# One-hot comparisons of a histogram shared between VectorE and GpSimd, and a hardware loop written out

## The chip, the cores and the metric

The kernel runs on one core of a Trainium2 chip. The metric is the device time of one execution in microseconds, as the median of several runs. Lower is better.

## The reference, cut to what matters

The program is a stack of four graph layers over 50,000 nodes and 25,000 edges. `src` and `dst` are the ends of each edge. The part that matters here is the degree count that the first layer asks for, and a row number for the compact tables:

```
loops = arange(n)
src   = concat([edge_index[0], loops])
deg   = segment_sum(ones, src, num_segments=n)
norm  = where(deg > 0, rsqrt(deg), 0)
```

Every later layer sums over `dst`. For that the kernel also needs to know, for each node, whether it has edges that end there, and its place among the nodes that have. So two histograms over the nodes are wanted: one of `src` (side 0) and one of `dst` (side 1).

## The kernel before, in words

The edges are padded to 25,600, which are T = 200 tiles of P = 128 edges. The function `prelude` is one stage of the program. It runs after the edge lists have been brought into SBUF (`edges_in`) and before the stage `node_rows`, whose first loads read what the prelude writes (`info_s`). Between two stages stands a barrier of all engines (in `run`, lines 2572 to 2580).

A histogram is computed as a sum of matrix products. A node number is split into a high part (number shifted right by 9, fewer than 98 values) and a low part (number and 511). For one tile and one side, the high parts become a one-hot matrix of 128 edges by 128 columns (`hi1`), and the low parts a one-hot matrix of 128 edges by 512 columns (`lo1`). Both are float16. TensorE multiplies the transposed first by the second and accumulates the 128x512 result in PSUM (`ph[:, side, :]`) over all tiles. Each one-hot matrix is one `tensor_scalar` with `is_equal`: a row of counting numbers (`g.iota_lo`, float16) against a value per partition, which is a column of `part` (float32, in SBUF).

Before, all four comparisons of a tile are made by VectorE, in the order hi side 0, lo side 0, hi side 1, lo side 1 (lines 500 and 501). The buffers `hi1` and `lo1` hold PER = 8 tiles. Two semaphores order the two engines: `s_cmp` counts finished pairs of comparisons, and TensorE waits for it before each product (line 539); `s_mm` counts finished products, and VectorE waits for it before it overwrites a buffer (line 499). Both engines run a hardware loop of 25 turns with 8 tiles written out in it. The counts in the semaphores are worked out from the loop register. GpSimd has no work in this stage.

After the loop TensorE closes the two sums (line 542), VectorE reads them (lines 504 and 505), and a chain of some 20 small steps over VectorE, ScalarE and TensorE makes the degree norm, a running count and the turned weights. The SP queue meanwhile loads weights, and at the end writes `info_s`.

`wait_alone(g, eng, sem, value)` is a wait followed by an increment of a semaphore that nobody waits for; it keeps the wait an instruction of its own.

Of the kernel before, what the change touches and what calls it, by code (L numbers as in the profile page):

```python
# [11 lines left out]
ALU = mybir.AluOpType  # L12
# [6 lines left out]
P = 128  # L19
# [3 lines left out]
T = EP // P  # L23
# [48 lines left out]
def wait_alone(g, eng, sem, value):  # L72

    eng.wait_ge(sem, value)
    eng.sem_inc(g.state.waits, 1)
# [315 lines left out]
def prelude(nc, g):  # L391
# [2 lines left out]
    s_ld, s_z, s_zd, s_big, s_bl, s_pe, s_v, s_d, s_w = (g.sem("wt_" + n) for n in ("ld", "z", "zd", "big", "bl", "pe", "v", "d", "w"))  # L394
    s_zh, s_cmp, s_mm, s_all, s_vec, s_deg, s_norm, s_sum, s_pre, s_row, s_out, s_turned = (
        g.sem("nn_" + n) for n in ("zh", "cmp", "mm", "all", "vec", "deg", "norm", "sum", "pre", "row", "out", "turned"))
    PER = 8
    with ctx:
        sb = lambda n, s, d=F32: ctx.enter_context(nc.sbuf_tensor(n, s, d))
# [9 lines left out]
        part = sb("nn_partf", [P, 2, 2, T])  # L409
# [36 lines left out]
        @block.sync  # L446
        def _(sp):
            for dest, src in loads:
                sp.dma_start(dest, src).then_inc(s_ld, 16)
            sp.wait_ge(s_z, 1)  # L450
            for k, a in ((2, g.vec1[:, 0]), (3, g.vec2[:, 0])):
                sp.dma_start(cols[0:HFULL, k, :], a[0:HFULL * HL].rearrange("(p w) -> p w", w=HL)).then_inc(s_vec, 16)
                sp.dma_start(cols[HFULL:HR, k, 0:HLEFT], a[HFULL * HL:N].unsqueeze(0)).then_inc(s_vec, 16)
            sp.dma_start(g.w1big_s, zero[:, 0:P]).then_inc(s_zd, 16)
            sp.dma_start(g.w2big_s.rearrange("(k p) n -> p k n", p=P), zero[:, P:3 * P].rearrange("p (k n) -> p k n", k=2)).then_inc(s_zd, 16)
            for dest, src in heads:
                sp.dma_start(dest, src).then_inc(s_ld, 16)
            sp.wait_ge(s_zd, 32)
            with nc.allow_non_contiguous_dma(reason="small weights laid out once"):
                for dest, src in pieces:  # L460
                    sp.dma_start(dest, src).then_inc(s_big, 16)
            sp.wait_ge(s_big, 16 * len(pieces))
            sp.dma_start(g.w1big[:, :], g.w1big_s).then_inc(s_bl, 16)
            sp.dma_start(g.w2big[:, :, :], g.w2big_s.rearrange("(k p) n -> p k n", p=P)).then_inc(s_bl, 16)
            sp.wait_ge(s_row, 1)
            sp.dma_start(g.info_s.rearrange("(p w) k -> p (w k)", w=HL), rows[:, :, :].rearrange("p w k -> p (w k)")).then_inc(s_out, 16)
            sp.wait_ge(s_w, 1)
            sp.dma_start(g.h_tab[EP:EP + 1, :], g.b0_row[0:1, :]).then_inc(s_d, 16)
            sp.wait_ge(s_out, 16)
            sp.wait_ge(s_d, 16)  # L470

        @block.scalar
        def _(a):
# [3 lines left out]
            a.wait_ge(s_norm, 1)  # L477
            a.activation(cols[:, 0, :], cols[:, 0, :], ACT.Exp, scale=-0.5).then_inc(s_norm, 1)

        @block.vector  # L480
        def _(v):
            v.memset(att[:, :, :], 0.0)
            v.memset(ones[:, :], 1.0)
            v.memset(cols[:, :, :], 0.0)
            v.memset(line[:, :], 1.0)
            v.memset(total[:, :], 0.0)
            v.memset(zero[:, :], 0.0).then_inc(s_z, 1)
            v.memset(zh[:, :], 0.0).then_inc(s_zh, 1)
            c = Chain(v, s_v)
            v.tensor_copy(both_i[:, 0, :], g.src_f[:, :])  # L490
            c.step(v.tensor_copy(both_i[:, 1, :], g.dst_f[:, :]))
            v.tensor_scalar(part_i[:, 0, :, :], both_i[:, :, :], 9, None, ALU.logical_shift_right)
            c.step(v.tensor_scalar(part_i[:, 1, :, :], both_i[:, :, :], HL - 1, None, ALU.bitwise_and))
            c.step(v.tensor_copy(part[:, :, :, :], part_i[:, :, :, :]))
            v.sem_inc(s_cmp, 2 * PER)
            with v.Fori(0, T // PER) as i:
                for k in range(PER):
                    for side in range(2):
                        v.wait_ge(s_mm, i * 2 * PER + 2 * k + side + 1)
                        v.tensor_scalar(hi1[:, k, side, :], g.iota_lo[:, 0:P], part[:, 0, side, bass.ds(i * PER + k, 1)], None, ALU.is_equal)  # L500
                        v.tensor_scalar(lo1[:, k, side, :], g.iota_lo[:, :], part[:, 1, side, bass.ds(i * PER + k, 1)], None,
                                        ALU.is_equal).then_inc(s_cmp, 1)
            v.wait_ge(s_all, 2)
            v.tensor_scalar(cols[:, 0, :], ph[0:HR, 0, :], 1.0, None, ALU.add).then_inc(s_deg, 1)
            c.step(v.tensor_copy(hist[:, :], ph[0:HR, 1, :]))
            v.tensor_reduce(total[0:HR, :], hist[:, :], AX.X, ALU.add).then_inc(s_sum, 1)
            v.wait_ge(s_pre, 1)
            c.step(v.tensor_copy(first[:, :], pp[0:HR, :]))
            c.step(v.tensor_tensor_scan(upto[:, :], line[:, :], hist[:, :], first[:, :], ALU.mult, ALU.add))
            c.step(v.scalar_tensor_tensor(cols[:, 1, :], hist[:, :], 0.5, upto[:, :], ALU.is_gt, ALU.mult))  # L510
            v.wait_ge(s_norm, 2)
            v.wait_ge(s_vec, 64)
            v.tensor_copy(rows[:, :, :].rearrange("p w k -> p k w"), cols[:, :, :]).then_inc(s_row, 1)
            v.wait_ge(s_ld, 16 * (len(loads) + len(heads)))
            c.step(v.tensor_scalar(g.b1_rows[:, :], g.b1_rows[:, :], 0.0, None, ALU.max))
            v.wait_ge(s_pe, 18)
            for n in range(18):
                turned = v.tensor_copy(wT[:, n, :], ps[:, n // 4, n % 4, :])
            turned.then_inc(s_turned, 1)
            v.wait_ge(s_bl, 32)  # L520
            v.tensor_scalar(g.w1big[:, :], g.w1big[:, :], float(1 / np.sqrt(MUL)), None, ALU.mult)
            v.tensor_scalar(g.w2big[S:2 * S, 0, :], g.w2big[S:2 * S, 0, :], float(1 / np.sqrt(3.0)), None, ALU.mult)
            c.step(v.tensor_scalar(g.wfc2[:, :], g.wfc2[:, :], float(1 / np.sqrt(HID)), None, ALU.mult))
            v.wait_ge(s_pe, 18 + 3)
            v.tensor_copy(g.wq[:, :], pq)
            v.tensor_copy(g.wa[:, :], pa)
            v.tensor_tensor(g.bu_rows[:, :], bu[:, :], pb, ALU.subtract)
            v.tensor_scalar(g.b0_row[0:1, :], p0, 0.0, None, ALU.max).then_inc(s_w, 1)

        @block.tensor  # L530
        def _(pe):
            pe.wait_ge(s_zh, 1)
            for side in range(2):
                pe.matmul(ph[:, side, :], zh[:, 0:P], zh[:, :], start=True, stop=False)
            pe.sem_inc(s_mm, 2 * PER)
            with pe.Fori(0, T // PER) as i:
                for k in range(PER):
                    for side in range(2):
                        pe.wait_ge(s_cmp, i * 2 * PER + 2 * PER + 2 * k + side + 1)
                        pe.matmul(ph[:, side, :], hi1[:, k, side, :], lo1[:, k, side, :], start=False, stop=False).then_inc(s_mm, 1)  # L540
            for side in range(2):
                pe.matmul(ph[:, side, :], zh[:, 0:P], zh[:, :], start=False, stop=True).then_inc(s_all, 1)
            pe.wait_ge(s_sum, 1)
            pe.matmul(pp, g.lower[:, :], total[:, :], start=True, stop=True).then_inc(s_pre, 1)
            pe.wait_ge(s_z, 1)
            pe.wait_ge(s_ld, 16 * (len(loads) + len(heads)))
            for n in range(16):
                pe.transpose(ps[:, n // 4, n % 4, :], g.wr[:, n, :], g.ident[:, :]).then_inc(s_pe, 1)
            for n in range(2):
                pe.transpose(ps[:, 4, n, :], g.w12[:, n * P:(n + 1) * P], g.ident[:, :]).then_inc(s_pe, 1)  # L550
            pe.wait_ge(s_turned, 1)
            for n in range(16):
                last = pe.matmul(pq[:, n:n + 1], wT[:, n, :], g.att_q[:, n // R_:n // R_ + 1], start=True, stop=True)
            last.then_inc(s_pe, 1)
            for k in range(2):
                last = pe.matmul(pa, wT[:, 16 + k, :], att[:, k, :], start=(k == 0), stop=(k == 1))
            last.then_inc(s_pe, 1)
            for k in range(2):
                pe.matmul(pb, ones[:, :], g.wu[:, k, :], start=(k == 0), stop=(k == 1))

            pe.matmul(p0, g.b1_col[:, 0:1], g.ident[:, :], start=True, stop=True).then_inc(s_pe, 1)
# [2078 lines left out]
```

## Time and profile before

| | |
|---|---|
| runs | 4418.27, 4420.27, 4423.72 us; median 4420.27 |
| profiled execution | 4440.37 us, its span 4438.7 us |
| mean granted TensorE clock in it | 0.821 of full speed |
| busy share of the span | VectorE 77%, TensorE 68%, ScalarE 49%, GpSimd 47% |
| the stage in question | about 45 to 244.8 us of the span; the histogram loop 50.8 to 220.9 us |

Busy shares are averages over many stages that have different limits. What a change in one stage is worth is read from the rows of that stage.

### The profile page before, as it was taken

The numbers are of one execution on the slowest core, as the hardware profiler recorded it, in microseconds if no ns is written. First come the engines' busy times: TensorE is split into PE (matmuls) and PEld (weight loads), VectorE is DVE, ScalarE is ACT, GpSimd is POOL, SyncE is SP. The second block draws the span as 40 slices with busy tenths as digits, with TensorE's granted clock in tenths as the row PEclk, the third lists the DMA queues.
The fourth block names the chain that finished last, engine by engine and source line by source line (L and its number), as shares of the span: only waits on it lengthen the run. The fifth ranks groups of instructions, "written<-read, shape, count | busy, mean of one in ns | idle before, by whom it ended". The sixth has DMA issues, their size and how long they took to land. (4 is left out here: it accounts for less than half of the span.)

```text
span 4438.7 us, 67467 instructions
## 1 busy us (share of the span) xinstructions
PE 3028.4 (68%) x12342; PEld 1728.7 (39%) x12342; DVE 3396.4 (77%) x9927; ACT 2153.8 (49%) x5600; POOL 2094.9 (47%) x2258
## 2 busy tenths in 40 slices
PE   5956644444445999478999224888886999706886
PEld 1255533333332444123444112555553666503443
DVE  6978858888886888675555685888884666697997
ACT  0057756776662222162222355766664666504554
POOL 0057767777774555006553002555544555203566
PEclk9967767677767999788999555989887999958998
DMA  2079967767773222174222496444444565503332
GB/s 51 2 210 285 286 207 230 230 223 228 230 225 89 64 62 61 40 229 86 60 62 47 131 245 164 116 118 122 118 120 131 196 200 194 170 0 112 113 112 87
DMA packets 621013, 627.71 MB, mean 141 GB/s; under 512 B 167332, under 2 KB 494590, under 8 KB 614468
## 3 DMA queue, kind: packets, MB, share of 16 engines
q1 hardware_dynamic: 572900, 523.78, 39.4%
q0 software_dynamic: 48000, 102.76, 9.6%
q14 instruction: 84, 0.69, 0.0%
q8 instruction: 29, 0.48, 0.0%
HBM read 333.97 MB, written 296.91 MB: 142 GB/s over the span
## 5 line engine op out<-in xcount | busy, mean ns | idle before, releaser
L1410 PE MATMUL r_pM<-r_masked,wr 128*128 128x512 f32 x1600 | 750.0, 622 | 55.2 <-DVE r_masked L1361 31.5
L1361 DVE SCALAR_TENSOR_TENSOR r_masked<-r_typ,r_hT 128x512 f32<-128x512 f32 x800 | 493.8, 689 | 241.4 <-ACT r_hT L1388 164.0
L1410 PEld LDWEIGHTS r_pM<-r_masked,wr 128*128 128x128 f32 x1600 | 308.7, 199 | 426.7 <-issue 326.1
L1252 PE MATMUL e_pY<-ident,e_agg 128*128 128x128 f32 x400 | 134.0, 438 | 370.3 <-issue 246.7
L741 POOL DMA_INDIRECT q_rows<-nr,row_x x200 | 258.0, 1290 | 209.4 <-PE q_pT L590 149.8
L2431 POOL DMA_INDIRECT out<-o_base,o_at_o x200 | 241.6, 1208 | 162.1 <-DVE o_base L2472 93.8
L741 POOL DMA_INDIRECT r_xs<-h_tab,r_at_s x200 | 216.1, 1080 | 87.7 <-issue 51.8
L741 POOL DMA_INDIRECT r_xs<-tab,r_at_s x200 | 214.1, 1071 | 89.1 <-issue 52.3
L1252 PEld LDWEIGHTS e_pY<-ident,e_agg 128*128 128x128 f32 x400 | 106.9, 327 | 382.3 <-issue 305.1
L590 PE MATMUL g_pT<-ident,g_hT 128*128 128x128 f32 x400 | 96.0, 384 | 226.5 <-ACT g_hT L1792 177.1
L1006 PE MATMUL na_pZ<-w,na_aT 128*128 128x128 f32 x784 | 159.6, 386 | 117.7 <-ACT na_aT L988 117.6
L741 POOL DMA_INDIRECT i_hs<-hr,i_at_s x200 | 194.5, 972 | 87.9 <-issue 50.4
L741 POOL DMA_INDIRECT e_zs<-xz,src_c x200 | 191.1, 955 | 70.1 <-issue 60.7
L2239 ACT ACTIVATE q_eo<-q_pO,b 128x512 f32<-128x512 f32 x196 | 134.8, 688 | 181.9 <-PE q_pO L2274 147.9
L741 POOL DMA_INDIRECT e_zd<-xz,dst_c x200 | 192.8, 964 | 53.5 <-issue 48.5
L1006 PEld LDWEIGHTS na_pZ<-w,na_aT 128*128 128x128 f32 x784 | 147.3, 289 | 131.0 <-ACT na_aT L988 113.1
L1388 ACT ACTIVATE r_hT<-r_pS 128x512 f32<-128x512 f32 x100 | 59.6, 596 | 273.8 <-PE r_pS L590 261.3
L2274 PE MATMUL q_pO<-q_nT,w 128*128 128x512 f32 x392 | 187.7, 602 | 5.2 <-issue 5.2
L590 PEld LDWEIGHTS g_pT<-ident,g_hT 128*128 128x128 f32 x400 | 61.6, 191 | 301.3 <-ACT g_hT L1792 118.3
L1098 POOL TENSOR_TENSOR e_zh<-e_z,e_hh 128x512 f32<-128x512 f32 x98 | 139.0, 1438 | 75.0 <-ACT e_hh L1201 60.8
L1903 POOL COPY i_at_s<-row_x 128x4 int32 (+1 forms) x50 | 9.4, 187 | 347.8 <-PEq L715 327.8
L2208 DVE TENSOR_TENSOR q_base<-q_pU,q_base 128x512 f32<-128x512 f32 x98 | 67.8, 692 | 132.5 <-PE q_pU L2283 121.0
(418 smaller groups left out, 9048.8 us busy)
## 6 DMA issues: line engine op xcount, KB each, us to landing
xz<-na_xz SPq DMA_DIRECT2D x49, 1040.0 KB
r_typ<-vec_s SPq DMA_DIRECT2D x100, 256.0 KB
g_al<-alpha_s SPq DMA_DIRECT2D x100, 256.0 KB, 3.9
na_xz<-in_x SPq DMA_DIRECT2D x49, 512.0 KB
tab<-na_x SPq DMA_DIRECT2D x49, 512.0 KB
e_xin<-tab SPq DMA_DIRECT2D x49, 512.0 KB
hr<-e_hh SPq DMA_DIRECT2D x49, 512.0 KB
zh_s<-e_zh SPq DMA_DIRECT2D x49, 512.0 KB
```

The lines of the kernel that those rows point to most:

```text
L590: last = pe.transpose(ps[:, j * P:(j + 1) * P], y4[:, j, :], g.ident[:, :])
L741: pool.indirect_dma_start(dest[:, j, :], None, table, bass.IndirectOffsetOnAxis(ap=index[:, j:j + 1], axis=0), element_offset=first).then_ ...
L1006: last = pe.matmul(pZ[p.slot(2)][m][:, j * P:(j + 1) * P], aT[:, m * J + j, :], g.w0[:, :], start=True, stop=True)
L1098: pool.tensor_tensor(zh[s][:, of(m), :], z[s][:, of(m), :], hh[s][:, of(m), :], ALU.add).then_inc(nd.zz, 1)
L1252: pe.matmul(pY[s][:, cols], agg[s][:, cols], g.ident[:, :], start=True, stop=False)
L1361: v.scalar_tensor_tensor(masked[:, r, :], typ[d.slot(4)][:, :], float(r), hT[d.slot(2)][:, :], ALU.is_equal, ALU.mult).then_inc(ev.mk, 1)
L1388: a.activation(hT[b.slot(2)][:, :], pS[b.slot(2)][:, :], ACT.Relu).then_inc(ev.hT, 1)
L1410: pe.matmul(pM[s][:, :], g.wr[:, layer * R_ + r, :], masked[:, r, :], start=(r == 0), stop=(r == R_ - 1)).then_inc(ev.mm, 1)
L2208: v.tensor_tensor(rows, four(pU[m][:, :]), rows, ALU.add).then_inc(nd.fo, 1)
L2239: a.activation(eo[:, m, k, :], pO[m][:, k, :], ACT.Exp, bias=g.b12[:, k:k + 1])
L2274: last = pe.matmul(pO[m][:, k, :], g.w12[:, k * P:(k + 1) * P], nT[:, of(m), :], start=True, stop=True)
L2431: pool.indirect_dma_start(g.out, bass.IndirectOffsetOnAxis(ap=at_o[s][:, j:j + 1], axis=0), base[s][:, j, :], None, bounds_check=N - 1, oo ...
```

## The change

GpSimd takes the narrow comparison of side 1 (`hi1[:, k, 1, :]`) of every tile. VectorE keeps hi side 0, lo side 0 and lo side 1. A semaphore `s_parts` tells GpSimd once that `part` is ready, and `s_hi` counts its comparisons. TensorE waits for `s_hi` as well before each product of side 1. The hardware loops on VectorE and TensorE become Python loops over all 200 tiles, so that every instruction is in the program once per tile, with constants for the semaphore values and for the column of `part`. GpSimd's part is written out in the same way. The number of buffers stays 8.

```diff
+    s_parts, s_hi = g.sem("nn_parts"), g.sem("nn_hi")
...
+        @block.gpsimd
+        def _(pool):
+            wait_alone(g, pool, s_parts, 1)
+            for t in range(T):
+                if t >= PER:
+                    wait_alone(g, pool, s_mm, 2 * (t - PER) + 2)
+                pool.tensor_scalar(hi1[:, t % PER, 1, :], g.iota_lo[:, 0:P], part[:, 0, 1, t:t + 1], None, ALU.is_equal).then_inc(s_hi, 1)
...
-            v.sem_inc(s_cmp, 2 * PER)
-            with v.Fori(0, T // PER) as i:
-                for k in range(PER):
-                    for side in range(2):
-                        v.wait_ge(s_mm, i * 2 * PER + 2 * k + side + 1)
-                        v.tensor_scalar(hi1[:, k, side, :], g.iota_lo[:, 0:P], part[:, 0, side, bass.ds(i * PER + k, 1)], None, ALU.is_equal)
-                        v.tensor_scalar(lo1[:, k, side, :], g.iota_lo[:, :], part[:, 1, side, bass.ds(i * PER + k, 1)], None,
-                                        ALU.is_equal).then_inc(s_cmp, 1)
+            v.sem_inc(s_parts, 1)
+            for t in range(T):
+                k = t % PER
+                for side in range(2):
+                    if t >= PER:
+                        v.wait_ge(s_mm, 2 * (t - PER) + side + 1)
+                    if side == 0:
+                        v.tensor_scalar(hi1[:, k, side, :], g.iota_lo[:, 0:P], part[:, 0, side, t:t + 1], None, ALU.is_equal)
+                    v.tensor_scalar(lo1[:, k, side, :], g.iota_lo[:, :], part[:, 1, side, t:t + 1], None, ALU.is_equal).then_inc(s_cmp, 1)
...
-            pe.sem_inc(s_mm, 2 * PER)
-            with pe.Fori(0, T // PER) as i:
-                for k in range(PER):
-                    for side in range(2):
-                        pe.wait_ge(s_cmp, i * 2 * PER + 2 * PER + 2 * k + side + 1)
-                        pe.matmul(ph[:, side, :], hi1[:, k, side, :], lo1[:, k, side, :], start=False, stop=False).then_inc(s_mm, 1)
+            for t in range(T):
+                k = t % PER
+                for side in range(2):
+                    if side == 1:
+                        pe.wait_ge(s_hi, t + 1)
+                    pe.wait_ge(s_cmp, 2 * t + side + 1)
+                    pe.matmul(ph[:, side, :], hi1[:, k, side, :], lo1[:, k, side, :], start=False, stop=False).then_inc(s_mm, 1)
```

## Rows read from the trace of the kernel before

**Rows 1.** Busy time in the histogram loop, by engine, then clock, DMA share, GB/s

```profile
50.80:221.20 170.40, 155.83 (x401) 38.34 (x402) 170.09 (x800) 0.00 (x0) 0.00 (x0) 1.00 0.07 9
```

**Rows 2.** Groups of instructions in the loop: busy us, mean ns, then idle before

```profile
L540 PE MATMUL nn_ph<-nn_lo,nn_hi 128*128 128x512 f16 x400 | 156.0, 395 | 15.5 <-DVE nn_lo L501 1.5
L501 DVE TENSOR_SCALAR nn_lo<-iota_lo,nn_partf 128x512 f16<-128x512 f16 x400 | 134.2, 335 | 0.0
L500 DVE TENSOR_SCALAR nn_hi<-iota_lo,nn_partf 128x128 f16<-128x128 f16 x400 | 94.9, 237 | 0.5 <-DVE nn_partf L494 0.5
...
L540 PEld LDWEIGHTS nn_ph<-nn_lo,nn_hi 128*128 128x128 f16 x400 | 38.3, 96 | 133.8 <-DVE nn_lo L501 133.2 <-issue 0.6
```

**Rows 3.** Timeline inside the loop: start us, duration us, instruction

```profile
100.11 0.24 DVE L500 TENSOR_SCALAR nn_hi<-iota_lo,nn_partf 128x128 f16<-128x128 f16 x1
...
100.27 0.34 DVE L501 TENSOR_SCALAR nn_lo<-iota_lo,nn_partf 128x512 f16<-128x512 f16 x1
100.53 0.23 DVE L500 TENSOR_SCALAR nn_hi<-iota_lo,nn_partf 128x128 f16<-128x128 f16 x1
```

**Rows 4.** Timeline of the SP queue's weight loads and of the loop's end

```profile
120.66 0.35 SPq L463 DMA_DIRECT2D w1big<-w1big_s  x1
...
221.17 0.59 PE L542 MATMUL nn_ph<-nn_zh 128*128 128x512 f16 x2
221.80 0.69 DVE L504 TENSOR_SCALAR nn_cols<-nn_ph 98x512 f32<-98x512 f32 x1 [0.92 <-PE nn_ph L542]
```

**Rows 5.** GpSimd's groups in the whole span, by form

```profile
L1909 POOL TENSOR_TENSOR i_total<-i_x,i_hh 128x512 f32<-128x512 f32 x50 | 63.4, 1267 | 163.2 <-ACT i_hh L2060 163.0
...
L899 POOL TENSOR_SCALAR na_q<-na_q 128x8 f32<-128x8 f32 x49 | 11.8, 240 | 9.7 <-POOL na_q L917 9.7
...
L917 POOL TENSOR_TENSOR na_q<-na_ss,na_nsq 128x8 f32<-128x8 f32 x49 | 9.9, 203 | 19.9 <-POOL na_nsq L914 18.5 <-ACT na_junk L972 1.4
...
L277 POOL TENSOR_SCALAR_AFFINE_SELECT lower<-lower 128x128 f32<-128x128 f32 x1 | 0.3, 294 | 0.1
L275 POOL MEMSET lower<- 128x128 f32 x1 | 0.2, 206 | 0.1
...
L895 POOL MEMSET na_half<- 128x8 f32 x1 | 0.1, 106 | 239.3 <-POOLq L2579 239.3
```

**Rows 6.** GpSimd's na_q at L919: ns min/median/max, then a timeline of one

```profile
L919 POOL TENSOR_SCALAR na_q<-na_q x49: 249/702/802, 268.8 to 620.1; 128x8 f32<-128x8 f32 x49
```
```profile
402.24 1.29 DVE L939 TENSOR_TENSOR na_y<-na_xz,na_mv 128x512 f32<-128x512 f32 x2
402.87 0.77 POOL L919 TENSOR_SCALAR na_q<-na_q 128x8 f32<-128x8 f32 x1 [0.20 <-POOL na_q L900]
```

**Rows 7.** VectorE's i_t at L1955: ns min/median/max, then a timeline of one

```profile
L1955 DVE TENSOR_TENSOR i_t<-i_ws,i_ya x50: 424/426/1512, 2754.0 to 3337.4; 128x256 f32<-128x256 f32 x50
```
```profile
2991.98 1.26 POOL L1912 TENSOR_TENSOR i_base<-i_total,bu_rows 128x512 f32<-128x512 f32 x1 [0.35 <-POOL i_total L1909]
2992.01 1.51 DVE L1955 TENSOR_TENSOR i_t<-i_ws,i_ya 128x256 f32<-128x256 f32 x1
```

**Rows 8.** VectorE's normalising tensor_scalar from SBUF (L584): ns min/median/max

```profile
L584 DVE TENSOR_SCALAR e_n<-e_hh,e_mvh,e_rh x392: 328/342/566, 663.6 to 1348.0; 128x128 f32<-128x128 f32 x196
```

**Rows 9.** Timelines of GpSimd beside two VectorE instructions in a row

```profile
261.53 1.29 DVE L939 TENSOR_TENSOR na_y<-na_xz,na_mv 128x512 f32<-128x512 f32 x2
261.69 0.63 POOL L899 TENSOR_SCALAR na_rs<-na_mv 128x8 f32<-128x8 f32 x1 [2.50 <-DVE na_mv L829]
```
```profile
998.24 1.28 DVE L1141 TENSOR_TENSOR e_z<-e_xin,b_rows 128x512 f32<-128x512 f32 x2
998.43 3.45 POOL L1098 TENSOR_TENSOR e_zh<-e_z,e_hh 128x512 f32<-128x512 f32 x2 [1.16 <-ACT e_hh L1201]
```

**Rows 10.** The same GpSimd instruction over the span: ns min/median/max

```profile
L1098 POOL TENSOR_TENSOR e_zh<-e_z,e_hh x98: 1257/1271/2215, 655.7 to 1340.9; 128x512 f32<-128x512 f32 x98
```

## The prediction

> **What bounds the kernel now.** I first asked for busy time in the stretch of the loop. VectorE is busy for 170.09 of 170.40 us, GpSimd does nothing, and TensorE has its full clock, which is the 2.4 GHz level [rows 1]. Then I read the groups of that stretch: VectorE has no idle time before either comparison, while TensorE's weight load waits 133.2 us for `nn_lo` [rows 2]. So VectorE alone sets the pace. The reader should see that a matmul's 395 ns are no limit: they overlap, and two of them at the loop's end take 0.59 us together, about 0.2 us apart [rows 4]. TensorE could do a tile in some 0.6 us. The timeline gives the price of one instruction on VectorE. A hi comparison starts at 100.11, the lo behind it at 100.27, the next hi at 100.53 [rows 3]. So a hi takes 0.16 us of VectorE and a lo 0.26 us, each less than its duration (237 and 335 ns [rows 2]) by some 73 ns, by which the next one overlaps. A tile is two of each. The 400 pairs fill 170.1 us, which is 425 ns a pair and 850 ns a tile.
>
> What stands behind the loop starts when the closing matmuls end (221.80 after 221.17 + 0.59 [rows 4]). The SP queue has issued the last weight loads at about 121 us [rows 4], 100 us before, so no transfer ends the loop's stretch, also if the loop gets 30 us shorter. The stages behind begin after a barrier and need `info_s`. So the time of the kernel moves by what the loop moves, one for one: 200 tiles, 0.2 us for each ns of a tile.
>
> **Removed from VectorE.** One hi comparison per tile, 163 ns: VectorE alone would need 850 - 163 = 687 ns for a tile, and the 200 tiles save 32.6 us. The loop's branch and register instructions go too; they run on the sequencer, VectorE shows no idle time from them [rows 2], so they are worth nothing. Waits and column addresses become constants, also nothing while VectorE's engine and not its sequencer is the limit; it stays so, for the sequencer gets fewer instructions per tile.
>
> **Added to TensorE.** One wait per tile on its sequencer, and the buffer of side 1 is filled by another engine. Matmuls are behind VectorE by less than a tile and GpSimd may be 8 tiles ahead, so this costs nothing unless GpSimd falls behind. If it does, TensorE stops at side 1, the matmul of side 0 of the next tile is queued behind it, and VectorE stops 8 tiles later for want of a buffer.
>
> **Written out.** VectorE gets about 1,000 instructions in a row, TensorE about 1,400, GpSimd about 600. The stretch of before has no such row of code. The bound below is nothing, since each instruction is fetched while its engine is busy with those before. For the bound above I have no near row; I put one gap like the 1.16 us before L1098 [rows 9] to every 50 tiles, which is 4.6 us. I take 0, the side that the gapless loop of rows 2 is nearer to, and keep 4.6 for the range. The Trainium skill ("Runtime: NRT & Kernel Launch", section "Instruction fetch mechanics") says that straight code is fetched ahead in order and that a branch out of the window is what stalls. By it the term is 0 as well or slightly below; no run here shows it yet.
>
> **Added to GpSimd: its own price.** No row has GpSimd doing `is_equal` on 128 float16 with a value per partition. Below: a `tensor_scalar` on 8 elements takes 240 ns [rows 5]. A memset goes from 106 to 206 ns for 120 elements more, 0.83 ns each; with that slope the comparison takes 240 + 100 = 340 ns. A `tensor_tensor` goes from 203 ns (8) to 1267 ns (512), 2.1 ns an element, which gives 240 + 253 = 493 ns. The affine select on 128 elements takes 294 ns. So 240 to 493 ns with 294 and 340 between. A read of the value per partition comes on top. I take the middle of 340 and 493, 415 ns. That is well below 687 ns, so GpSimd by itself is not the bound.
>
> **Added: the two engines meet at SBUF.** This decides. GpSimd's `na_q` at L919 takes 249 ns when alone and 702 in the median. In the timeline it starts at 402.87, VectorE's pair of `tensor_tensor` ends at 402.24 + 1.29 = 403.53, and it ends at 403.64, 110 ns later [rows 6]. So it had done 249 - 110 = 140 ns of its work and then stood still until VectorE was through. The other way round it is the same: L1955 needs 424 ns, but when GpSimd's L1912 had started 30 ns before, it took 1.51 us and ended 280 ns after L1912's end (2993.52 against 2993.24) [rows 7]; it too stood still after its first 142 ns. One keeps the other out for nearly its whole instruction. The instructions of rows 6 and 7 have two SBUF inputs. The comparisons have one, but 384 elements more cost 98 ns [rows 2], 0.26 ns each, four elements a cycle where those go one in 1.04 ns; and VectorE's `tensor_scalar` from SBUF at L584 is stretched from 342 up to 566 ns at times [rows 8], so that kind is kept out too. The Trainium skill ("SBUF — State Buffer", section "Who interferes with whom") says so as a rule: GpSimd has no port but VectorE's second pair, `tensor_scalar` in its fast modes holds it for the whole instruction, and the other is blocked. The traces of L919 and L1955 agree.
>
> The price follows. Between two VectorE instructions in a row the port is free for 142 - 73 = 69 ns. A GpSimd instruction of duration D needs it for D - 140. If it gets in at the boundary, VectorE is late by D - 209 ns: with D = 415 by 206 ns, and the tile takes 687 + 206 = 893 ns. With D = 340 it is 818, with D = 493 it is 971, with 294 it is 772. The even point with 850 ns is D = 372.
>
> It need not get in. L899 waited for one of two VectorE instructions and ended at 262.32, about 0.1 us after the first (261.53 + 0.69, a single one being half of the 1.29 and the overlap), with the pair not longer than that of rows 6 [rows 9]. L1098 on the other hand took 2215 ns in its worst case [rows 10], the one at 998.43, which is until 1.13 us after both had ended [rows 9]: VectorE's second passed it. If that is the rule, VectorE runs until its 8 buffers are used up and then stands still: 275 ns for the rest of GpSimd's instruction, 395 ns for the matmul [rows 2] and 80 ns for two hand-overs (40 ns lie between 221.76 and 221.80 [rows 4]), 750 ns in all. In that time GpSimd gets two instructions done, 375 ns each; or a third, if it takes the port just ahead of VectorE, which then ends its hold 275 + 2 x 415 - 142 = 963 ns after the start, 321 ns each. So 321 to 375 ns a tile instead of 206, and a tile of 1008 to 1062 ns, 1035 in the middle. I take the first case for most tiles, and go a quarter of the way to the second: 893 + 0.25 x 142 = 928 ns. The sum is (928 - 850) x 0.2 = +15.6 us on the loop of 170 us. The profiled execution of before took 4440.4 us around a span of 4438.7, 20 us over the median of the runs. All terms are differences within the loop, which ran evenly, so by its own time the sum is 4456.0, and against the median of the runs it is 4420.3 + 15.6 = **4435.9 us**.
>
> **The rivals.**
> (a) Even: GpSimd's comparison takes 330 to 390 ns and always gets in at the boundary. The slope of memset and the affine select speak for it, the read of the value per partition against it. The tile is 808 to 868 ns, the kernel 4412 to 4424 us, 4418 in the middle. The Trainium skill ("GPSIMD Engine Reference", section 4.1) calls one-input work on GpSimd roughly line-rate, which would be this rival; rows 5 neither confirm nor exclude it for this form.
> (b) Faster, the other side: the comparison does not hold VectorE up, because it is short and its share of the port fits between two instructions, as L899's did [rows 9], or because this form does not take the port. The tile is then 687 ns, set by VectorE, and the kernel 4420.3 - 32.6 = 4388 us. It decides once D is under some 325 ns (tile under 806). Against it stand L584 and the 128 elements, 16 times what L899 has.
> (c) VectorE passes GpSimd at nearly each boundary: 1008 to 1062 ns a tile, +32 to +42 us, 4452 to 4463 us. For it stands L1098, which was passed in its worst case; against it that L1098 reads two tensors and is three times as long.
>
> **How the numbers follow.** Forecast 0.43, (a) 0.24, (b) 0.15, (c) 0.18. A change under 0.2% (8.8 us, 44 ns a tile) can't be told from none. (b) counts as faster and 0.05 of (a)'s edge with it: faster 0.20. The rest of (a) and a little of the forecast's lower edge: same 0.24. The forecast and (c): slower 0.56. The range reaches from (a) down to D of about 310 ns, a tile of 788 ns and -12 us, and somewhat into (b), up to the end of (c): 4400 to 4463 us. It leaves out most of (b) and, above, (c) with a cost of fetching on top.
>
> **What the profile after would show.** VectorE's records: hi x200, lo x400 in the loop, the median durations at 236 and 334 ns if they are not held, longer for one in three if GpSimd gets in, and all short with gaps in a bunch if it is passed. GpSimd: 200 `tensor_scalar`, the minimum is D, the median tells how long it is kept out. VectorE's idle time before `nn_lo`: near zero in the forecast, 60 to 75 us waiting for TensorE in (c). The loop's length: 137 us in (b), 162 to 174 in (a), 186 in the forecast, 202 to 212 in (c). TensorE's clock should stay at 1.00 with this many columns. The prediction is wrong if D is far under 370 ns, if the port is not shared by this form, or if gaps that end with no releaser show on an engine at equal distances (code).

## The result, and the profile after

The changed kernel takes 4405.73 us in the median (4403.01 to 4410.78, 8 runs), the kernel before in the same sets 4419.27 us (4411.91 to 4428.84, 8 runs). The ratio is 0.9967, 95% interval 0.9955 to 0.9978: faster by 0.33%, or 10 to 20 us. Forecast were 4435.9 us, slower, and a range of 4400 to 4463. The time lies in the range and the direction is the wrong one.

The groups of the loop after, which answer to [rows 2] (busy us, mean ns, then idle before and its cause):

```profile
L487 POOL TENSOR_SCALAR nn_hi<-iota_lo,nn_partf 128x128 f16<-128x128 f16 x200 | 158.9, 813 | 45.3 <-DVEq L504 45.3
L512 DVE TENSOR_SCALAR nn_lo<-iota_lo,nn_partf 128x512 f16<-128x512 f16 x400 | 138.6, 386 | 0.0
L551 PE MATMUL nn_ph<-nn_lo,nn_hi 128*128 128x512 f16 x400 | 128.8, 392 | 31.3 <-POOL nn_hi L487 24.9 <-DVE nn_lo L512 1.2
L511 DVE TENSOR_SCALAR nn_hi<-iota_lo,nn_partf 128x128 f16<-128x128 f16 x200 | 54.3, 271 | 0.1
L551 PEld LDWEIGHTS nn_ph<-nn_lo,nn_hi 128*128 128x128 f16 x400 | 38.3, 96 | 122.4 <-POOL nn_hi L487 96.5 <-DVE nn_lo L512 20.9
```

And a timeline of two tiles on VectorE, answering to [rows 3]:

```profile
119.12 0.79 DVE L512 TENSOR_SCALAR nn_lo<-iota_lo,nn_partf 128x512 f16<-128x512 f16 x2
119.83 0.27 DVE L511 TENSOR_SCALAR nn_hi<-iota_lo,nn_partf 128x128 f16<-128x128 f16 x1
120.00 0.60 DVE L512 TENSOR_SCALAR nn_lo<-iota_lo,nn_partf 128x512 f16<-128x512 f16 x2
120.52 0.27 DVE L511 TENSOR_SCALAR nn_hi<-iota_lo,nn_partf 128x128 f16<-128x128 f16 x1
120.71 0.78 DVE L512 TENSOR_SCALAR nn_lo<-iota_lo,nn_partf 128x512 f16<-128x512 f16 x2
```

VectorE still has no idle time. A lo lasts 386 ns in the mean (335 before), a hi 271 (237 before). These durations alone don't show a loss, for in the run with ScalarE below a hi lasts 267 ns and no time is lost; the distance from start to start shows it. Two lo in a row take 0.60 us undisturbed and 0.79 when GpSimd keeps VectorE out. Tiles go in pairs, 119.83 to 120.52 to 121.42: one tile takes 0.69 us, which is what VectorE needs alone, and the next 0.90. GpSimd's comparisons take 676 and 947 ns in turn, 813 in the mean. So one comparison in two costs VectorE about 212 ns and the other nothing, and the loss of 106 ns a tile (793 - 687) is a mean. TensorE's weight loads now wait for GpSimd, 96.5 us in all. The first hi starts at 50.8 and the last at 208.7, so 199 tiles take 157.9 us, 793 ns each against 850 before and 928 forecast.

### The profile page after: what moved, and what is told of

It is laid out like the page before. It is cut to its first block and busy times, and to the rows that moved or that the text cites. A ratio compares the mean times of both kernels' runs of the same rounds, so it can differ in the third digit from the quotient of the medians.

```text
span 4401.3 us, 66157 instructions
## 1 busy us (share of the span) xinstructions
PE 2995.1 (68%) x12342; PEld 1721.8 (39%) x12342; DVE 3371.7 (77%) x9727; ACT 2153.3 (49%) x5600; POOL 2259.6 (51%) x2458
## 5 line engine op out<-in xcount | busy, mean ns | idle before, releaser
L1109 POOL TENSOR_TENSOR e_zh<-e_z,e_hh 128x512 f32<-128x512 f32 x98 | 161.0, 1662 | 51.1 <-ACT e_hh L1212 51.1
L487 POOL TENSOR_SCALAR nn_hi<-iota_lo,nn_partf 128x128 f16<-128x128 f16 x200 | 158.9, 813 | 45.3 <-DVEq L504 45.3
```

The lines of the kernel that those rows point to most:

```text
L487: pool.tensor_scalar(hi1[:, t % PER, 1, :], g.iota_lo[:, 0:P], part[:, 0, 1, t:t + 1], None, ALU.is_equal).then_inc(s_hi, 1)
L1109: pool.tensor_tensor(zh[s][:, of(m), :], z[s][:, of(m), :], hh[s][:, of(m), :], ALU.add).then_inc(nd.zz, 1)
```

## The experiments

Each execution's loop length is read from its own profile, which agrees within 0.2 us between executions of one kernel. Whole times vary more, and from chip to chip: the kernel before had medians of 4419.27, 4441.19 and 4417.12 us in three sets. So kernels that were executed once are compared by stages.

### Only written out

All four comparisons are VectorE's again, the loops stay written out, GpSimd's block is gone.

```diff
-                    if side == 0:
+                    if True:
                         v.tensor_scalar(hi1[:, k, side, :], ...
...
-                    if side == 1:
-                        pe.wait_ge(s_hi, t + 1)
```

> VectorE makes all four comparisons of a tile as before; only the loops of VectorE and TensorE are written out, and GpSimd has no part. Theory 1 (writing out is worth nothing, the gain is the comparison that left VectorE): the loop takes 170.1 us, 850 ns a tile, with durations of 236 and 334 ns. Rival (writing out by itself made each instruction cheaper or dearer, and hides in the difference): the loop differs by more than 2 us; at 165 us it would have given half of the 11 us that the loop gained.

Measured: the first hi starts at 50.8, the last at 220.4, as before to 0.1 us. So writing out is worth nothing in the loop, and the 57 ns a tile that were gained come from the comparison that moved. But the kernel took 4480.45 us, 57 more than the run of before beside it. The time is in a stage that the edit doesn't touch, the first layer's edges (busy times of the stage, then clock, DMA share, GB/s; this kernel, and the changed kernel):

```profile
624.70:1446.40 821.70, 305.63 (x1300) 230.66 (x1300) 621.19 (x2969) 491.06 (x1689) 541.97 (x498) 0.69 0.61 196
```
```profile
615.80:1359.20 743.40, 307.42 (x1300) 231.40 (x1300) 617.57 (x2969) 490.82 (x1690) 542.45 (x498) 0.70 0.68 216
```

The work is the same, and the stage is 78 us longer than in the changed kernel (before's is 747 us). Its chain of waits on VectorE names no other engine (us in total, times, longest):

```profile
DVE e_agg L1126 <- issue: 45.3, 10, 5.6
...
DVE e_nn L1116 <- issue: 35.2, 9, 4.1
```

Together 80 us, twice in each turn of that stage's hardware loop, 4 to 5 us each; the same two waits are 1.8 and 2.4 us in the changed kernel. The DMA queue that brings instructions had 66 packets and 0.54 MB in the stage here, and 21 packets and 0.17 MB in the changed kernel:

```profile
q14 instruction: 66, 0.54, 0.2%
```
```profile
q14 instruction: 21, 0.17, 0.1%
```

This reads as VectorE fetching the same code anew in each turn. It is inferred: the queue's packets don't name the engine that they are for.

### Back in place, and out of place

Two kernels ask whether it is the place of the later code. The first is the one above with 57 small memsets into a spare tile in front of it on VectorE: its later code then lies 256 instructions behind that of the changed kernel. The second is the changed kernel with 199 such memsets.

```diff
             v.memset(att[:, :, :], 0.0)
+            for n in range(57):
+                v.memset(fill[:, n:n + 1], 0.0)
```

> The kernel with all comparisons on VectorE and loops written out, which took 57 us more than before although its loop took the same 170 us: 78 us of it lie in the stage of the first layer's edges, where VectorE stands 4 to 5 us twice in each turn of its loop. Here 57 small memsets into a spare tile stand in front of it on VectorE, so that VectorE's later code sits 256 instructions behind its place in the changed kernel, and not 199. Theory P (the place of the later loop's code in VectorE's instruction stream decides whether it is fetched anew in each turn, and places 256 apart are alike): that stage goes back from 822 to about 744 us, and the kernel to 4420 us give or take 15, with 3 us for the memsets. Rival (it is the sheer length of the code, or some state of those executions): it stays at about 822 us and 4480.

> The changed kernel with 199 small memsets in front of the loop on VectorE, so that VectorE's later code lies where it lay in the written-out kernel without GpSimd. They cost some 9 us before the loop. Theory P: the stage of the first layer's edges goes from 743 to about 822 us, with some 66 packets of instructions in it in place of 21, and the kernel takes 75 to 90 us more than the changed kernel beside it. Rival (place is not the cause): 745 us.

Measured: 747.8 us for the stage with 57 memsets, the histogram loop unchanged at 169.6 us for 399 pairs. The kernel took 4432.84 us beside a before of 4441.19, within the 4420 give or take 15 that were expected, and it is no longer the slower one. With 199 memsets in the otherwise unchanged kernel:

```profile
619.90:1442.00 822.10, 305.75 (x1300) 229.96 (x1300) 620.01 (x2969) 490.87 (x1689) 540.50 (x498) 0.68 0.60 196
```

The queue again brought 66 packets in that stage. The kernel took 4471.44 us against 4410.73 for the changed kernel beside it: 61 more, not 75 to 90, for the interaction stage gave 16 us back (613 against 630, with TensorE's granted clock at 0.88 against 0.84). So the place of VectorE's code decides and not its length, and 256 instructions on VectorE put it back.

### GpSimd's price, measured alone

VectorE waits once, until GpSimd has made its first 8 comparisons.

```diff
             v.sem_inc(s_parts, 1)
+            v.wait_ge(s_hi, PER)
             for t in range(T):
```

> The changed kernel, but VectorE waits until GpSimd has made its first 8 comparisons. They show the duration D of GpSimd's comparison with nobody beside it. Theory 1 (the step that failed is D: the rule D - 209 ns holds, and D is smaller than the 415 ns taken): the loop of the changed kernel stands at 793 ns a tile, 106 over 687, so D should be 315 ns. Theory 2 (D is as predicted or longer, and the step that failed is the rule: GpSimd doesn't hold the port for all of its instruction): D is 380 ns or more. The rest of the loop runs at 793 ns a tile for both.

```profile
50.81 4.67 POOL L487 TENSOR_SCALAR nn_hi<-iota_lo,nn_partf 128x128 f16<-128x128 f16 x8 [45.12 <-DVEq L504]
...
57.33 8.33 POOL L487 TENSOR_SCALAR nn_hi<-iota_lo,nn_partf 128x128 f16<-128x128 f16 x4 [1.85 <-PE nn_ph L552]
```

Eight take 4.67 us, about 590 ns each (the shortest of the run is 591). That is beyond the range of 240 to 493 ns in which the prediction put it. Theory 2 holds: with D = 591 the rule of D - 209 asks for 382 ns a tile, and VectorE loses 106. The second row shows the next ones, made beside a VectorE that runs without a wait: four took 8.33 us, over 2 us each. That is rival (c), GpSimd passed at one boundary after the other. It cost VectorE little: two tiles in three took 688 ns and the third 750, so 62 ns for each comparison. It lasted until VectorE stood for a buffer (558 ns); then the tile settled at 793 ns again, over tiles 40 to 180. The kernel took 4409.58 us beside a before of 4423.60.

### The same work with nobody waiting for it

VectorE makes all four; GpSimd makes its comparisons as well, into a buffer that nobody reads.

```diff
-                pool.tensor_scalar(hi1[:, t % PER, 1, :], ...
+                if t >= PER:
+                    wait_alone(g, pool, s_hi, t - PER + 1)
+                pool.tensor_scalar(spare[:, t % PER, :], ...
```

> VectorE makes all four comparisons, loops written out; GpSimd makes its 200 comparisons as well, at the same pace, into a buffer that nobody reads, and TensorE waits for VectorE alone. The rest is as in the changed kernel. So a GpSimd comparison costs here only what it keeps VectorE from. Theory 1 and 2 (contention at SBUF, 106 ns a comparison): the loop takes 170 + 21 = 191 us. Rival (the 106 ns a tile come from the hand-over, TensorE waiting for the comparison that comes late from GpSimd, and VectorE for its buffer): 170 us.

```profile
L490 POOL TENSOR_SCALAR nn_spare<-iota_lo,nn_partf 128x128 f16<-128x128 f16 x131 | 164.2, 1272 | 46.3 <-DVEq L507 45.4 <-PE nn_ph L552 0.9
```

The loop went from 51.0 to 231.0 us, 180 us and not 191. GpSimd's comparisons took 1272 ns each, so only some 144 fell into the loop, and they cost VectorE (180 - 169.6) / 144, about 70 ns each. Contention is shown: nobody waits for GpSimd here and VectorE still loses. Within the loop there are two patterns. At first GpSimd makes a comparison every 607 ns, two a tile, and the tile takes 1213 ns, so each costs 181 ns. After some 15 of them it is kept out longer, one comparison takes 1356 ns, and the tile takes 891 to 892, so each costs about 62 ns. The size of the loss goes by how the two engines fall against each other. The kernel took 4507.01 us, 83 more than the run of before beside it: the stage of the first layer's edges is 77 us longer (824 us, with 66 packets of instructions) because of its place, the prelude 23, since its loop is longer and GpSimd still has comparisons to make behind it, and the interaction gives back some 17 (617 us).

### One thing less to read, and fewer columns

In the first kernel GpSimd compares with a constant, so the second histogram leaves out the high part; in the second kernel it compares 98 columns. Both make the first 8 alone.

```diff
-                pool.tensor_scalar(hi1[:, t % PER, 1, :], g.iota_lo[:, 0:P], part[:, 0, 1, t:t + 1], ...
+                pool.tensor_scalar(hi1[:, t % PER, 1, :], g.iota_lo[:, 0:P], 3.0, ...
```
```diff
+            pool.memset(hi1[:, :, 1, :], 0.0).then_inc(s_clean, 1)
...
-                pool.tensor_scalar(hi1[:, t % PER, 1, :], ...
+                pool.tensor_scalar(hi1[:, t % PER, 1, 0:HR], g.iota_lo[:, 0:HR], part[:, 0, 1, t:t + 1], ...
```

> As the run with the first 8 alone, but GpSimd compares with the constant 3.0 in place of the value per partition, so it reads one thing less; the second histogram is wrong in its high part. Theory A (GpSimd's instruction touches the port twice, once for the value and once for the row, and each costs VectorE a wait): D falls by 60 ns or more, and VectorE's excess over 687 ns a tile falls from 106 to about half. Theory B (the value per partition costs nothing to speak of): D and the loop stay within 10 ns.

> GpSimd compares 98 columns in place of 128 (the others stay zero; no high part is over 97), and its first 8 comparisons run alone. Alone they took 591 ns with 128 columns and 516 with a constant in place of the value per partition. Theory H (GpSimd's time goes by the element, some 1.7 ns each behind a fixed part near that of the 8-element rows): D falls by 50 ns or more, to about 540. What VectorE loses falls only if it is kept out for the length of GpSimd's work: then 793 ns a tile falls by about as much, to 740. Rival K (it is kept out for GpSimd's short touches of the port, whatever their length): the tile stays within 20 ns of 793.

The groups of the second in its loop:

```profile
L490 POOL TENSOR_SCALAR nn_hi<-iota_lo,nn_partf 128x98 f16<-128x98 f16 x200 | 145.0, 744 | 6.5 <-DVEq L507 4.6 <-PE nn_ph L555 1.8
...
L516 DVE TENSOR_SCALAR nn_lo<-iota_lo,nn_partf 128x512 f16<-128x512 f16 x400 | 122.3, 346 | 0.6 <-PE nn_ph L555 0.6
L515 DVE TENSOR_SCALAR nn_hi<-iota_lo,nn_partf 128x128 f16<-128x128 f16 x200 | 49.8, 249 | 4.5 <-POOL nn_hi L490 4.4
```

Alone, both take 516 ns: reading the value costs GpSimd 75 ns, and 30 columns less save 75 ns, 2.5 ns a column. From tile 40 to 180, when it ran evenly, the tile took 720 ns with the constant and 694 with 98 columns, so VectorE lost 33 and 7 ns. Of the two theories on the constant A is the nearer: D falls by 75 ns and the loss by more than the half that it named, to a third. It is not shown that the read of the value made up the rest of the loss, for with 98 columns that read is still there and the loss is smaller yet. Neither H nor K holds for the columns: D fell by 75 ns, as H has it, but the loss by 99. Two comparisons with the same D of 516 ns cost 33 and 7 ns, so D alone does not fix the loss. In both kernels each tile loses the same, where with the full comparison every second tile loses 212 ns and the others nothing. The kernels took 4394.20 us (before beside it 4423.60) and 4406.23 us (before 4441.19).

### ScalarE in GpSimd's place

```diff
+            a.wait_ge(s_parts, 1)
+            for t in range(T + 1):
+                if t < T:
+                    if t >= PER:
+                        a.wait_ge(s_mm, 2 * (t - PER) + 2)
+                    a.activation(far[:, t % PER, :], g.iota_lo[:, 0:P], ACT.Square, bias=minus[:, t:t + 1]).then_inc(s_far, 1)
+                if t:
+                    a.wait_ge(s_far, t)
+                    a.activation(hi1[:, (t - 1) % PER, 1, :], far[:, (t - 1) % PER, :], ACT.Relu, bias=g.ones_col[:, :], scale=-1.0).then_inc(s_hi, 1)
```

`minus` holds the high parts times -1, one instruction of VectorE's before the loop.

> ScalarE makes the narrow comparison of side 1 in place of GpSimd, in two steps: the square of (number - value), then Relu(1 - that). GpSimd has no part. Theory 1 (the 106 ns over 687 in each tile are SBUF contention between VectorE and GpSimd): VectorE's tile takes 687 ns, the loop 138 us, 21 us less than with GpSimd, and the two ScalarE steps take about 0.3 us each, 0.6 us a tile, just below. Rival (ScalarE's two steps with their waits take more than 687 ns, or slow TensorE): the loop is as long as ScalarE's pace makes it, 150 us or more. The kernel: 4420 - 32 = 4388 us, if the later stages' code is placed well.

```profile
L484 ACT ACTIVATE nn_far<-iota_lo,nn_minus 128x128 f16<-128x128 f16 x200 | 79.6, 399 | 4.4 <-DVEq L509 4.4
L487 ACT ACTIVATE nn_hi<-nn_far,ones_col 128x128 f16<-128x128 f16 x200 | 77.1, 386 | 0.0
L516 DVE TENSOR_SCALAR nn_hi<-iota_lo,nn_partf 128x128 f16<-128x128 f16 x200 | 53.4, 267 | 0.1
```

VectorE's first hi starts at 50.7 and its last at 187.5: 687 ns a tile, what VectorE alone needs by [rows 3]. The comparison that comes from another engine costs VectorE nothing here. With the run above, where nobody waits for GpSimd and VectorE loses all the same, the 106 ns are contention between VectorE and GpSimd. The kernel took 4406.16 us beside a before of 4441.19.

### Both helpers

ScalarE makes the comparison of side 0 as above, GpSimd that of side 1, VectorE the two lo.

> ScalarE makes the narrow comparison of side 0 (square, then Relu of 1 minus it), GpSimd that of side 1, VectorE only the two wide ones. Theory 1: VectorE's tile is 526 ns plus what GpSimd keeps it from, 106 ns, so 632 ns, 126 us for the loop and 4420 - 44 = 4376 us; GpSimd at 591 ns alone is then slowed to about the same pace. Rival (GpSimd, which needs 591 ns alone and 677 to 948 beside VectorE, becomes the bound): 700 to 800 ns a tile, the loop 140 to 160 us, no better than ScalarE alone.

GpSimd runs without a pause at 677 ns a comparison: 51.6 to 182.7 us, 659 ns a tile, between the two theories. VectorE has no idle time either (0.1 us), though its two lo need some 526 ns alone (0.26 us each by [rows 3]). So neither waits for the other's result and each slows the other; that one of them alone sets the pace is not shown. The kernel took 4430.75 us in the median of 12 (before 4441.19, 17 runs), ratio 0.9974, interval 0.9959 to 0.9989, although the loop is 39 us shorter than before's. The stage of the first layer's edges was 782 us long, with 66 packets of instructions: VectorE's code had moved by some 200 instructions again, the other way this time. Only one of the two waits is there, 28 us in 9 turns, so the packets tell that such a loss is there and not how large it is.

So the next one has 98 columns on both helpers and 198 memsets on VectorE in front of a wait of 9 us late in the stage, which put its later code back.

```diff
+            for n in range(198):
+                v.memset(fill[:, n:n + 1], 0.0)
             v.wait_ge(s_pe, 18 + 3)
```

> ScalarE makes the narrow comparison of side 0 and GpSimd that of side 1, both on the 98 columns that can be hit; VectorE makes the two wide ones. 198 small memsets on VectorE, late in the stage where it stands idle for 9 us, put its later code back where the changed kernel has it. GpSimd alone takes 516 ns at 98 columns. Theory 1 (GpSimd beside VectorE sets the pace): 516 ns and what it waits at the port, 560 to 620 ns a tile, the loop 112 to 124 us, the kernel 46 to 58 us under before. Rival (VectorE sets it with its 526 ns and a wait of 50 ns): 576 ns, 115 us. With the first layer's edges at 745 to 752 us; if the place is missed, 780 to 822.

```profile
L528 DVE TENSOR_SCALAR nn_lo<-iota_lo,nn_partf 128x512 f16<-128x512 f16 x400 | 122.8, 385 | 0.1
L504 POOL TENSOR_SCALAR nn_hi<-iota_lo,nn_partf 128x98 f16<-128x98 f16 x200 | 122.8, 633 | 4.1 <-DVEq L522 4.1
L568 PE MATMUL nn_ph<-nn_lo,nn_hi 128*128 128x512 f16 x400 | 122.1, 388 | 2.2 <-ACT nn_hi L490 1.8
```

The loop takes 122 us, 614 ns a tile, which is in the range of theory 1 (560 to 620); again neither GpSimd nor VectorE pauses. The later stage takes 746 us. The kernel takes 4365.35 us (4361.11 to 4372.56, 4 runs) against 4417.12 (7 runs): ratio 0.9879, interval 0.9856 to 0.9901. The changed kernel took 4410.73 us beside it, so it beats both kernels.

### Both kernels again, on one chip

> The kernel before once more, for a second profile of it on the chip of the three runs beside it. If the 16 us by which the stage at 3368 us was longer in the first profile of before (498 against 483 us in the changed kernel's) are the chip's and not the kernel's, it is as long here as in the changed kernel's run beside it. The loop: 170.1 us.

> The changed kernel once more, beside before on one chip. The loop is again 158.9 us. Theory (nothing but the loop is gained): the other stages are as long as before's within 3 us each, and the whole is 11 us shorter. Rival (some later stage, that of the first layer's edges or of the interaction, gains by where its code now lies): one of them is shorter by 4 us or more again, as in the first pair of profiles (747 to 743 us and 633 to 626 us).

4428.32 and 4410.73 us. The prelude is 199.6 and 188.3 us long, 11.3 less. The stages behind the interaction, at 3372 and 3354 us, are equal (483.0 and 482.7): the 498 us of the first profile of before were not the kernel's. Four other kernels, all run on one chip, had 494 to 499 us there. The first layer's edges: 746.7 and 744.7. The interaction is 637 us before and 630 after, as in the first pair (633 and 626). So of the expectations for the changed kernel the rival holds for this stage: it is over 4 us shorter again. The stage moves with TensorE's granted clock:

```profile
2735.00:3372.00 637.00, 545.96 (x2400) 313.48 (x2400) 497.41 (x1851) 412.85 (x902) 333.78 (x350) 0.83 0.43 114
```

That is before; the changed kernel has 0.84 there, the displaced one 0.88 and 613 us. All three kernels that have VectorE's later code 199 instructions behind that of the changed kernel, or nearly so, took 613 to 617 us there, and all others 623 to 637. That speaks for the place bearing on this stage too, in the other direction. Why, and what moves the clock, was not tried.

## Why the prediction was wrong

**What bounds the loop, and one for one.** Right. The stage after the prelude began 11.0 us earlier in the first pair (244.9 and 233.9), as the loop ended 11.0 us earlier.

**Removed, 163 ns a tile.** Right. Without contention the tile is 687 ns (the run with ScalarE).

**GpSimd's own price, 415 ns.** Mis-sized: 591 ns. The slopes of memset and `tensor_tensor` did not bound it from above. Between 98 and 128 columns a comparison costs GpSimd 2.5 ns a column, and its value costs 75 ns.

**The two engines meet at SBUF: D - 209 ns, 206 ns a tile.** This is the step that failed. That they meet was right. That GpSimd needs the port for all of its time but 140 ns was read off instructions with two inputs and long bodies [rows 6, 7] and does not hold for this one: by it 591 ns would have cost 382, and it cost 106 in the mean, 212 and nothing in turn, or 7 with 98 columns. No steady pattern in any run cost more than 212. So GpSimd did not keep VectorE out for the whole of its instruction. The two errors worked against each other: with the right D the same rule would have given 1069 ns a tile and 4464 us, and that the time fell into the range is luck. Where exactly in its 591 ns GpSimd takes the port, and what decides between the patterns, is not shown. This failure was not among the prediction's signs of being wrong, which looked for a D far under 370 ns or a port that is not shared.

**Passed at the boundary, a quarter of the way.** It happens: over 2 us a comparison behind the first 8, and 1272 ns where nobody waits for it. In the changed kernel the two fell into step from the first tiles, one comparison a tile, GpSimd at 676 to 949 ns. VectorE never stood for a buffer. So the term of 35 ns was nothing. Where GpSimd was passed, VectorE lost some 62 ns a comparison, which the prediction did not count.

**Writing out, 0 with a bound of 4.6 us.** In the loop 0, shown. The bound was wrong in kind: the cost of moved code lies in a later loop and was 78 us in one place and nothing in another. That the changed kernel lies well is luck, since nothing in the edit or the prediction saw to it. The Trainium skill ("Runtime: NRT & Kernel Launch", section "Instruction fetch mechanics") says that a taken branch out of the fetched window stalls. The runs fit it for the later loop, with 9 or 10 turns of two stalls of 4 to 5 us.

**The rest.** 11.3 us of the 13.5 between the medians (10 to 20 by the interval) are the prelude's. The other 2 are within what the interval allows; the interaction's 7 us in both pairs are seen, and their cause is open. Rival (b), the other side, named the right direction with a chance of 0.15 and the wrong size: its 32.6 us need GpSimd to cost VectorE nothing, and even with 98 columns it costs 7 ns.

## What to carry to other kernels

Before half an engine's work goes to GpSimd, measure one such instruction alone and beside VectorE: neither its duration nor what VectorE loses could be had from other forms. Where ScalarE is idle, try it too: it did the same work here in two steps, within the 687 ns of a tile, and VectorE lost nothing. And when code is written out or cut, compare every later stage: a hardware loop far behind can pay more than the edit gains, and more packets on the instruction queue (66 against 21 here) tell it.

## What the runs showed of the hardware that was not expected

A hardware loop on VectorE lost 78 us in 10 turns when 199 instructions came in front of it, and lost nothing with 256; the queue that brings instructions had 66 packets in place of 21. GpSimd takes 591 ns for a comparison of 128 float16 with a value per partition, 516 for 98, and 516 for 128 with a constant. In the even part of the loop VectorE loses 106, 7 and 33 ns a tile to these. The loss goes by the pattern as well: the same comparison of 591 ns cost 0 and 212 ns in turn, 181 ns, or 62 ns.
